# Four of the eight attention heads: maximum subtracted on GpSimd, one exponential on ScalarE, sums on VectorE; the score split over two slots

## The reference

```python
h = input @ W
s1 = jnp.einsum('bif,hf->bhi', h, a1)
s2 = jnp.einsum('bjf,hf->bhj', h, a2)
e = jax.nn.leaky_relu(s1[:, :, :, None] + s2[:, :, None, :] + a_b[None, :, None, None])
att = jnp.where(adj[:, None, :, :] > 0, e, NEG_INF)
att = jax.nn.softmax(att, axis=-1)
h_prime = jnp.einsum('bhij,bjf->bif', att, h) / att.shape[1]
```

## Time and profile before

| | us |
|---|---|
| median of 3 runs | 2086.39 (2083.98 to 2087.57) |
| the profiled execution's own time | 2077.1 |
| its span | 2075.3 |
| TensorE busy | 1737.3 (84%) |
| VectorE busy | 1727.0 (83%) |
| ScalarE busy | 1390.1 (67%) |
| GpSimd busy | 597.2 (29%) |

### The profile page before, as it was taken

How to read it: one execution, slowest core, us unless ns; L and a number is a source line. 1 busy time by engine, 2 the same in 40 slices (tenths; PEclk the granted TensorE clock), 3 DMA queues, 4 the chain that set the end, 5 groups by cost and what they waited for, 6 DMA issues and landing times. The chain is left out here.

```text
span 2075.3 us, 43855 instructions
## 1 busy us (share of the span) xinstructions
PE 1737.3 (84%) x13771; PEld 1096.7 (53%) x13771; DVE 1727.0 (83%) x2689; ACT 1390.1 (67%) x3229; POOL 597.2 (29%) x449
## 2 busy tenths in 40 slices
PE   2966777777776899897799999999999678988886
PEld 1855556555663666665465555555555234444445
DVE  5878888888875777785799999999999577888887
ACT  0533333333334999895588888888888687888884
POOL 1530000000002544443344444444444211111110
PEclk9989998999887999997999999999999899999999
DMA  6000000000000000000055555555555699999993
GB/s 183 1 13 1 1 0 0 0 0 0 0 1 4 7 6 4 6 6 21 32 224 223 222 222 223 220 223 220 223 220 223 256 371 350 391 376 369 375 342 88
DMA packets 123567, 292.98 MB, mean 141 GB/s; under 512 B 21376, under 2 KB 57608, under 8 KB 123288
## 3 DMA queue, kind: packets, MB, share of 16 engines
q1 hardware_dynamic: 106360, 283.37, 35.9%
q10 hardware_dynamic: 16896, 8.39, 1.4%
q0 software_dynamic: 256, 0.56, 0.1%
HBM read 150.45 MB, written 141.82 MB: 141 GB/s over the span
## 5 line engine op out<-in xcount | busy, mean ns | idle before, releaser
L1316 POOL TENSOR_TENSOR pair_ring<-hd 128x2048 f32 (+1 forms) x64 | 269.5, 4211 | 310.1 <-DVE pair_ring L1341 310.1
L1401 ACT ACTIVATE v_hid<-v_psW 128x1024 f32<-128x1024 f32 x256 | 263.2, 1028 | 84.9 <-PE v_psW L1439 84.9
L771 DVE TENSOR_REDUCE m_part<-m_psS 128x128 f32<-128x2048 f32 (+1 forms) x128 | 258.9, 2023 | 66.1 <-PE m_psS L638 66.1
L1337 DVE TENSOR_TENSOR pair_ring<-v_psX,hd 128x2048 f32<-128x2048 f32 x128 | 292.3, 2289 | 17.1 <-PE v_psW L1439 17.1
L1439 PE MATMUL v_psW<-pair_ring,p_w1T 128*64 128x512 f32 x1024 | 288.5, 596 | 0.0
L1404 ACT ACTIVATE v_junk<-v_psW 128x1024 bf16<-128x1024 f32 x256 | 263.0, 1027 | 0.0
L638 PE MATMUL m_psS<-m_onehot,m_tableT 32*128 32x128 f32 x3584 | 151.8, 307 | 127.7 <-DVE m_part L771 123.4
L1439 PE MATMUL v_psW<-pair_ring,l_w1T 128*64 128x512 f32 (+1 forms) x1024 | 252.5, 587 | 0.0
L1430 PE MATMUL v_psW<-p_ends,v_weights 128*64 128x512 bf16 x1536 | 235.2, 381 | 3.1 <-DMA v_fold<-in_c_fold_dram 3.1
L638 PEld LDWEIGHTS m_psS<-m_onehot,m_tableT 32*128 32x128 f32 x3584 | 128.6, 207 | 147.3 <-issue 78.2
L708 ACT ACTIVATE m_tableT<-m_psTT 128x512 f32<-128x512 f32 (+1 forms) x128 | 69.3, 541 | 202.4 <-PE m_psTT L620 202.1
(11 more groups left out here) (260 smaller groups left out, 3354.9 us busy)
## 6 DMA issues: line engine op xcount, KB each, us to landing
pair_hidden<-v_hid SPq DMA_DIRECT2D x256, 512.0 KB, 2.6
pair_ring<-pair_hidden SPq DMA_DIRECT2D x128, 1024.0 KB, 7.7
adj_ring<-in_adj_dram ACTq DMA_DIRECT2D x16, 256.0 KB, 5.5
x_all<-in_x_dram ACTq DMA_DIRECT2D x16, 256.0 KB, 5.5
out_dram<-x_all SPq DMA_DIRECT2D x16, 256.0 KB, 2.3
pair_scores<-s_rot SPq DMA_DIRECT2D x64, 32.0 KB, 4.6
s_fwd<-pair_scores SPq DMA_DIRECT2D x64, 32.0 KB, 3.9
s_wide<-pair_scores SPq DMA_DIRECT2D x64, 32.0 KB, 5.0
```

The costliest lines, as they stand in the source:

```text
L771: nc.vector.tensor_reduce(part[:, i % 2, r, :], psS[:, :, 0:w].rearrange("z q (c i) -> z i q c", i=N), AX.XY, ALU.max).then_inc(reduced, 1)
L1316: nc.gpsimd.tensor_tensor(D[:, home(u, SLABS - 1), :].rearrange("c (h d i) -> c h d i", h=2, i=N), one, far, ALU.subtract).then_inc(psub_d ...
L1337: nc.vector.tensor_tensor(slab(s), own, windows(hd, n, s)[1], ALU.max).then_inc(max_done, 1)
L1401: nc.scalar.activation(hid[:, s, :], psW[:, buf, :], ACT.Identity, accum_out=hsum[:, bass.ds(m, 1)]).then_inc(evacuated, 1)
```

## The change

`OWN = 4` heads keep the way of before. For the other four, GpSimd adds the negated maximum in place to the scores (a new instruction at the head of its slot, before the scaling), ScalarE takes one exponential over 512 columns without bias or accumulator output, and VectorE sums the four heads' rows ahead of the reciprocal. Two semaphores are new: `lowered` (GpSimd to ScalarE, and to VectorE, whose maximum writes the buffer that GpSimd reads) and `zsummed` (VectorE's sum to its reciprocal). The four splits are cut in two: the first two stay in slot 1, the last two go to slot 2.

```diff
@@ -496,6 +496,7 @@
 HC = HEADS * N
 ROWS = 3 * HEADS
 KR = ROWS + 3
+OWN = 4
 S2 = 32
 SR = S2 + HEADS
 
@@ -865,8 +866,8 @@
         sem = lambda name: k.sem("a_" + name)
         transposed, relued, h_mm, h_ready, s_mm, s_split = (sem(n) for n in (
             "transposed", "relued", "h_mm", "h_ready", "s_mm", "s_split"))
-        placed, e_mm, e_copied, leaky, negmax, expd = (sem(n) for n in (
-            "placed", "e_mm", "e_copied", "leaky", "negmax", "expd"))
+        placed, e_mm, e_copied, leaky, negmax, lowered, expd, zsummed = (sem(n) for n in (
+            "placed", "e_mm", "e_copied", "leaky", "negmax", "lowered", "expd", "zsummed"))
         recip, scaled, att_mm, att_ready, out_mm, added = (sem(n) for n in (
             "recip", "scaled", "att_mm", "att_ready", "out_mm", "added"))
         b = lambda i: slice(i * N, (i + 1) * N)
@@ -903,7 +904,8 @@
 
             @block.gpsimd
             def _(pool):
-                pool.sem_inc(scaled, BIAS)
+                for s in (lowered, scaled):
+                    pool.sem_inc(s, BIAS)
 
                 def normal(g, p):
                     pool.wait_ge(transposed, done(g - 2))
@@ -911,6 +913,11 @@
 
                 def slot(g, p, i, behind, ahead):
                     n = g * G + i
+                    if behind(2):
+                        pool.wait_ge(negmax, done(n - 2))
+                        upper = eu[:, i % 2, OWN * N:HC].rearrange("n (h j) -> n h j", j=N)
+                        nc.gpsimd.tensor_tensor(upper, upper, nmx[:, i % 2, OWN:HEADS].unsqueeze(2).broadcast_to([N, HEADS - OWN, N]),
+                                                ALU.add).then_inc(lowered, 1)
                     if behind(3):
                         at = (i - 3) % G
                         pool.wait_ge(recip, done(n - 3))
@@ -1008,10 +1015,11 @@
                         at = (i - 2) % G
                         act.wait_ge(att_mm, done(m - G))
                         act.wait_ge(recip, done(m - G))
-                        for h in range(HEADS):
-                            last = nc.scalar.activation(ex[:, at, b(h)], eu[:, i % 2, b(h)], ACT.Exp,
-                                                        bias=nmx[:, i % 2, h:h + 1], accum_out=zs[:, at, h:h + 1])
-                        last.then_inc(expd, 1)
+                        for h in range(OWN):
+                            nc.scalar.activation(ex[:, at, b(h)], eu[:, i % 2, b(h)], ACT.Exp,
+                                                 bias=nmx[:, i % 2, h:h + 1], accum_out=zs[:, at, h:h + 1])
+                        act.wait_ge(lowered, done(m))
+                        nc.scalar.activation(ex[:, at, OWN * N:HC], eu[:, i % 2, OWN * N:HC], ACT.Exp).then_inc(expd, 1)
                     if behind(0):
                         act.wait_ge(e_mm, done(n))
                         act.wait_ge(expd, done(n - 2))
@@ -1026,7 +1034,7 @@
 
             @block.vector
             def _(dve):
-                for s in (s_split, leaky, negmax, recip, att_ready, added):
+                for s in (s_split, leaky, negmax, zsummed, recip, att_ready, added):
                     dve.sem_inc(s, BIAS)
                 def split_scores(g, p, placed_before=True):
                     dve.wait_ge(s_mm, done(g))
@@ -1036,6 +1044,8 @@
                     dve.wait_ge(s_split, done(4 * g))
                     nc.vector.scalar_tensor_tensor(out=rest[:, :], in0=psF[0:SR, :], scalar=ab[:, 0:1], in1=parts[:, p, 0, :],
                                                    op0=ALU.add, op1=ALU.subtract).then_inc(s_split, 1)
+
+                def split_rest(g, p):
                     dve.wait_ge(s_split, done(4 * g + 1))
                     nc.vector.tensor_copy(parts[:, p, 1, :], rest[:, :]).then_inc(s_split, 1)
                     dve.wait_ge(s_split, done(4 * g + 2))
@@ -1056,6 +1066,9 @@
                         dve.wait_ge(expd, done(m))
                         at = (i - 3) % G
                         dve.wait_ge(scaled, done(m - G))
+                        nc.vector.tensor_reduce(zs[:, at, OWN:HEADS], ex[:, at, OWN * N:HC].rearrange("n (h j) -> n h j", j=N), AX.X,
+                                                ALU.add).then_inc(zsummed, 1)
+                        dve.wait_ge(zsummed, done(m))
                         nc.vector.reciprocal(rz[:, at, :], zs[:, at, :]).then_inc(recip, 1)
                     if behind(4):
                         m = n - 4
@@ -1069,13 +1082,17 @@
                                                        op0=ALU.mult, op1=ALU.add).then_inc(leaky, 1)
                         dve.wait_ge(leaky, done(m))
                         dve.wait_ge(expd, done(m - 2))
+                        dve.wait_ge(lowered, done(m - 2))
                         nc.vector.tensor_reduce(nmx[:, odd, :], eu[:, odd, :].rearrange("n (h j) -> n h j", j=N), AX.X, ALU.max,
                                                 negate=True).then_inc(negmax, 1)
                     if i == 1 and ahead(1):
                         split_scores(g + 1, 1 - p)
+                    if i == 2 and ahead(1):
+                        split_rest(g + 1, 1 - p)
                     if i == 3 and behind(4):
                         finish(g - 1)
                 split_scores(0, 0, placed_before=False)
+                split_rest(0, 0)
                 graphs(dve, slot)
 
 
```

## The result

| | before | changed |
|---|---|---|
| median (20 runs each) | 2081.75 us | 2094.32 us |
| lowest to highest | 2071.26 to 2091.66 | 2077.58 to 2110.54 |
| profiled execution, own time (span) | 2077.1 (2075.3) | 2110.54 (2108.7) |
| first to last finishing add of the stage | 278.9 us | 291.7 us |
| first matmul to last finishing add of the stage | 323.4 us | 340.6 us |

What follows compares the result with a forecast made beforehand. The ring through VectorE, GpSimd and TensorE was taken to bound the heads stage. Terms 0.61 + 0.73 - 0.6 + 0.5 = 1.24 us a quad, 15 quads, gave +19 us, from 2086.4 to 2105; range 2090 to 2123.

Steps and rivals of the forecast that it cites:

- The bound: Attention-heads stage: a ring of waits through VectorE, GpSimd and TensorE sets the pace; ScalarE's saving is costed at nothing.
- The ring: VectorE reciprocal, GpSimd scaling, TensorE sum, VectorE copy and later work: 18.66 us per quad (four graphs) at full clock.
- The first rival: Eight small exponentials in the heads stage: ScalarE sets the pace, so -12 us, 2074; chance 0.07.
- The ring's sum: Changed ring per quad of four graphs: 9.25 + 4.54 + 5.48 = 19.27 us, 0.61 us longer, without the meeting.
- The sum's 0.72 us: VectorE's new 128x512 sum ahead of each reciprocal: 0.686 us plus some 0.03 us, on the ring twice a quad.
- the splits' gain on the ring: The last two of four score splits, 1.06 us, leave the ring and go behind the next slot's maxima.
- The meeting: Slot 3's GpSimd subtraction and slot 2's moved VectorE splits exclude each other at SBUF: 0.73 us more per quad.
- The rival in which the two pass each other: Moved splits and GpSimd's subtraction do not delay each other: +7 to +14 us, 2093 to 2100; chance 0.2.
- the clock: TensorE's idle places lower its clock: slot 2 gains 0.6 us a quad, slot 0 costs 0.5 us.
- the slow sums: TensorE's slot 2 sums at lower clock behind idle time: 3.40 us against 2.05, in eight of twelve quads before.
- The rival in which the clock falls twice in every quad: The clock falls in both TensorE idle places, slots 2 and 0, of every quad: +36 us, 2122; chance 0.12.
- The transfer: SyncE's bounce of the scores through memory starts later but lands in time for TensorE: costed at nothing, cover about 1 us.

Runs made afterwards that it cites:

- scalar_freed: split_only with four heads' exponentials in one instruction without maxima, their sums never taken; ratio to the kernel before 0.9865.
- split_only: The kernel before with only the last two of the four splits moved behind slot 2's maxima; 2059.73 us against 2078.87, ratio 0.9912.
- short_sum: The changed kernel with VectorE's new sum reading 4 columns instead of 512; 2067.18 us, ratio to before 0.9952.
- no_subtract: The changed kernel without GpSimd's subtraction, the exponentials of four heads leaving the maximum out; ratio to before 1.0022.
- heads_only: The changed kernel with the last two splits back in slot 1, so only the heads are handed over; 2117.16 us, ratio to before 1.0201.
- own6: The changed kernel with two heads handed over instead of four (OWN = 6); ratio to before 0.9947.
- own6_again: The same kernel as own6, run again; 2063.26 us, ratio to before 0.9932.
- after_again: The changed kernel itself, run and profiled a second time; ratio to before 1.0097.
- sum_first: The changed kernel with the last two splits moved between slot 3's sum and its reciprocal; 2080.63 us, ratio to before 1.0043.
- before_filled: The kernel before with four unused extra matmuls filling TensorE's idle time ahead of slot 2's sum; ratio to before 0.9967.
- split_filled: split_only with four extra matmuls ahead of slot 2's sum; 2055.74 us against 2057.41 without them, ratio to before 0.9902.

## Why the prediction was right in kind, and where its size was off

**The bound was right.** The ring from reciprocal to scaling to head sum to copy set the pace, and ScalarE's saving was worth nothing: 41.5 us of waiting stand before its exponentials. Its signs came true as well: VectorE is 91% busy between 700 and 900 us, and the two reciprocals of the ring are 9.15 and 10.72 us apart (9.3 and some 10.7 were named). The first rival, ScalarE as the pace, is refuted for this kernel, and scalar_freed shows the reason: 3.7 us freed give 0.4 even in the best case. It holds in a way for split_only alone, where ScalarE's work (17.77 us by its rows) and the ring (8.53 + 9.07 = 17.60) are as good as equal.

**The ring's sum was near.** Predicted 20.0 us for a clean quad with the meeting, read off a long quad of before (18.66); measured 19.87 for the long one (9.15 + 5.15 + 5.57) and 18.68 for before. So +1.34 was predicted and +1.19 came. The sum's 0.72 us (0.71 from its start to the reciprocal's) is seen in the rows, its three times per quad in short_sum (the prediction says twice in words and counts three in its sum), and the splits' gain on the ring in split_only.

**The meeting was right, step by step.** 0.73 us was predicted, and 0.73 is what no_subtract gives back; the split's own growth is 0.68. Counted from the start of the maxima, 789.16 us, the prediction had the subtraction's end at 2.47 us and the last split's at 3.00; measured are 2.44 and 2.99. The cast was not delayed, as predicted. The sizes had come from rows of other shapes in other stages, so that they fit to 0.03 us is in part luck. The rival in which the two pass each other is refuted by L1052's 1.363 us. The rule of the Trainium skill ("SBUF — State Buffer", "Who interferes with whom") that a reduction never takes part agrees: beside GpSimd's work L1086 kept its 1.22 us and L1069 its 0.67.

```profile
784.27 1.04 POOL L313 TENSOR_TENSOR a_xn<-x_all,ln_negmean 128x512 f32 x1
...
786.48 1.04 POOL L919 TENSOR_TENSOR a_eu<-a_eu,a_nmx 128x512 f32<-128x512 f32 x1
```

```profile
784.35 1.22 DVE L1086 TENSOR_REDUCE a_nmx<-a_eu 128x8 f32<-128x1024 f32 x1
...
786.92 0.67 DVE L1069 TENSOR_REDUCE a_zs<-a_ex 128x4 f32<-128x512 f32 x1
```

**The term that was mis-sized is the clock.** The prediction had +1.24 us per quad; the mean of the twelve quads grew by 0.58 and 0.65 us in the two profiles. The ring was 0.15 too long in it, and the rest is the slow sums. The prediction put them at 0.3 us a quad for the old place and 0.5 for the new one, 0.8 in all against 0.90 before, a gain of 0.1. Measured (mean less clean) are 0.25 and 0.31 us against 0.86 before, a gain of 0.6.

What one slow sum costs was right. In slot 2 a quad with one is 0.2 to 0.6 us longer than its clean neighbours, since VectorE's longer way hides the rest (0.39 was predicted), and in slot 0 it is 1.5 to 1.6 us longer, unhidden (1.35 was predicted). Wrong was how many come. The idle time ahead of slot 2's sum did not stay at 1.33 us, it fell to 1.13, and in the two profiles of the changed kernel one and three of twelve sums there were slow, not eight. heads_only, where it stays at 1.3, has its eight again, so it is the moved splits that shortened it. In slot 0 the idle time came in two pieces as predicted, but of up to 0.61 + 0.70 us and not 1.6, and two of twelve sums were slow in each profile, not four in ten. That TensorE stood 0.5 to 0.7 us in this slot before the change too, without a slow sum, the prediction left out. The rival in which the clock falls twice in every quad is refuted; its nearest likeness is heads_only, which the moved splits prevent.

**The total came nearer than its terms, by luck.** Twelve quads at +1.24 us would be 15 us, and 7.0 and 7.8 us were measured. The ends of the stage, which the prediction counted as three quads (3.7 us), grew by 10.1 and 7.2 us: 4.3 and 4.0 up to the first finish, 5.8 and 3.2 in the last three quads, where some sums are slow too. The two errors partly cancel: 17.1 and 15.0 us for the whole stage, against 19 predicted.

**The transfer was right, narrowly.** TensorE waited for the scores once in 200 us, 0.2 us; in split_only, where the quad is shorter, eleven times and up to 0.9 us.

```profile
PE a_psE L962 <- DMA a_rhs<-head_scores: 0.2, 1, 0.2
```

**Not settled:** why the same code ahead of the heads takes different times. The heads begin at 637.54 us in the profile of before and at 648.02 and 646.63 in the two of the changed kernel. This is no habit of a kernel: own6 and own6_again, one and the same kernel, begin at 652.74 and 642.60. It goes with the granted clock of the first 637 us, 0.90 in before, 0.88 in both profiles of the changed kernel, 0.86 in own6 and 0.89 in own6_again. What lowers it there is open. It adds some microseconds of chance to every whole time, and so to the ratios.

## What to carry to other kernels

Ask of a busy engine whether the pace hangs on it before taking work off it: ScalarE, 98% busy in split_only, gave back a tenth of what it was freed of, and VectorE, the engine that took part of its work over, stood on the ring. Split a change that has two parts: here one part gains 0.9 to 1.0% and the other, put on top of it, costs 1.5 to 2%, and the version with only the splits moved (2057 to 2060 us) beats both kernels. When work moves to GpSimd, look at which VectorE instruction lies beside it: a two-input subtraction paid here in one order and a cast in the other, while reductions did not.

## What the runs showed of the hardware

- A sum is slow more often the longer TensorE idled just before it. Slow sums in twelve quads: behind 1.33 us, eight (before), and behind 1.31 to 1.32, eight (heads_only); behind 1.13 us one, three, three and five (changed, after_again, no_subtract, sum_first); behind 0.86 us none (own6 and own6_again); behind 0.69 none (short_sum); behind the 0.47 of before_filled none. Where it was 1.13 and not 1.33 us, three to seven sums fewer were slow in this slot, 0.3 to 0.8 us a quad.
- The length just before is not all that decides. In slot 0 sums were slow behind 0.70 us (two in changed, two in after_again, one each in sum_first, own6 and own6_again), behind 0.50 (split_filled) and behind 0.39 (sum_first), and each of these nine had a second idle piece of 0.2 to 0.8 us, 2 to 3 us earlier. With such a piece most sums were still not slow (none in heads_only and no_subtract); without one, as in the slot 0 of before and before_filled, none was. That the earlier piece is the cause was not tested. The granted clock between 700 and 900 us went with the number of slow sums: 0.88 in heads_only, 0.97 in the changed kernel, 1.00 in split_only.
- The record of a VectorE or GpSimd instruction that the other one holds up includes the wait, so no idle time shows it: the split went from 684 to 1363 ns when it was issued 0.28 us into the subtraction, the subtraction from 1040 to 1140 when it came 0.16 us behind a cast of 0.41. Which of VectorE's instructions pays hangs on the order: the split, when the cast was issued 0.16 us ahead of the subtraction (changed), and the cast, when it was issued 0.56 us (heads_only, 848 ns) or 0.43 us (sum_first, 858 ns) behind its start.
- In every second quad VectorE pauses 0.31 us ("issue") behind the finish, and that quad is 0.4 us longer at the same work; the loop's body holds two quads. What the pause is the profiles do not show. Two neighbouring quads must be read before one is called the length of the ring.
